# Last expert of a mixture-of-experts block: all weight blocks over three token tiles, then all over two

## What is computed

```python
capacity = max(1, int(CF * N / E))                       # 640
disp = jnp.zeros((E, capacity + 1, D)).at[se, pos].set(xf[st])[:, :capacity]
g = jnp.einsum('ecd,edf->ecf', disp, wg)                 # D = 256, F = 1024
u = jnp.einsum('ecd,edf->ecf', disp, wu)
eo = jnp.einsum('ecf,efd->ecd', jax.nn.silu(g) * u, wd)
contrib = gathered * (sw * keep)[:, None]
out = jnp.zeros_like(xf).at[st].add(contrib)             # x = x + gate * out
```

## Time and profile before

| | us |
|---|---|
| median of 3 runs | 678.95 (678.22 to 679.12) |
| the profiled execution's own time | 678.13 |
| its span, first to last instruction | 676.04 |
| TensorE busy | 568.7 (84%) |
| VectorE busy | 456.5 (68%) |
| ScalarE busy | 320.0 (47%) |
| GpSimd busy | 269.0 (40%) |

### The profile page before, as it was taken

The page is one execution under the profiler, slowest core; times in us unless marked ns, Lnnn a source line. Parts: engine busy times, 40 slices in busy tenths (PEclk is TensorE's granted clock), DMA queues, the critical chain, the costliest instruction groups (busy, mean ns, idle before and its releaser), DMA issues.

```text
span 676.0 us, 13788 instructions
## 1 busy us (share of the span) xinstructions
PE 568.7 (84%) x4041; PEld 529.4 (78%) x4041; DVE 456.5 (68%) x1304; ACT 320.0 (47%) x717; POOL 269.0 (40%) x427
## 2 busy tenths in 40 slices
PE   4999889998997101279999999999999999999990
PEld 3577668887776000169999999999999999999990
DVE  3577889897677877867756766567667666666431
ACT  3688778886444500034534534445345444454330
POOL 5688757776678000302007025043070160442304
PEclk9999999999999555569989999999999999999996
DMA  5322268545554900144408317344174073340203
GB/s 164 94 64 78 71 194 264 189 145 162 157 190 153 264 0 0 40 133 133 133 1 213 94 44 170 95 141 102 61 198 106 18 194 95 110 102 9 32 1 39
DMA packets 91911, 75.24 MB, mean 111 GB/s; under 512 B 12108, under 2 KB 88278, under 8 KB 91864
## 3 DMA queue, kind: packets, MB, share of 16 engines
q1 hardware_dynamic: 82872, 58.77, 28.6%
q0 software_dynamic: 8992, 15.90, 11.2%
HBM read 52.48 MB, written 22.16 MB: 110 GB/s over the span
## 4 chain that ended last, share of the span: by engine, by line
PE 59%; DVE 13%; issue 7%; POOL 3%; ACT 2%; DMA 2%; DVEq 1%; SPq 0%; ACTq 0%; POOLq 0%
PE bank L1329 33%; PE bank L1341 15%; PE bank L1247 3%; PE bank L1292 2%; DVE hit L880 2%; PE bank L1150 2%; PE bank L1306 1%; DMA mod_all<-mod_store 1%; DVE x L847 1%; DVE st L849 1%; POOL out L506 1%; PE bank L1227 1%; PE bank L1236 1%; DMA xg<-h_rows,g_idx 1%; PE bank L1202 0%
## 5 line engine op out<-in xcount | busy, mean ns | idle before, releaser
L1329 PE MATMUL bank<-xT_h,w_h 128*128 128x320 f32 x512 | 160.2, 313 | 2.3 <-DVE xT_l L1027 1.7
L1329 PE MATMUL bank<-xT_l,w_h 128*128 128x320 f32 x512 | 159.2, 311 | 0.4 <-issue 0.4
L1329 PE MATMUL bank<-xT_h,w_l 128*128 128x320 f32 x512 | 159.0, 311 | 0.0
L496 POOL DMA_INDIRECT xg<-h_rows,g_idx x40 | 43.8, 1095 | 274.5 <-DVE g_idx L999 264.7
L1055 DVE TENSOR_TENSOR hid<-act_g,bank 128x320 f32<-128x320 f32 x128 | 62.0, 484 | 74.1 <-ACT act_g L648 59.6
L652 ACT CAST hid_h<-hid 128x320 fp32r<-128x320 f32 x128 | 58.9, 460 | 97.5 <-DVE hid L1055 92.8
L648 ACT ACTIVATE act_g<-bank 128x320 f32<-128x320 f32 x128 | 55.8, 436 | 103.3 <-PE bank L1329 96.2
L1329 PEld LDWEIGHTS bank<-xT_h,w_h 128*128 128x128 f32 x512 | 97.6, 191 | 3.0 <-DVE w_l L1013 2.1
L1329 PEld LDWEIGHTS bank<-xT_h,w_l 128*128 128x128 f32 x512 | 97.5, 190 | 0.5 <-issue 0.5
L1329 PEld LDWEIGHTS bank<-xT_l,w_h 128*128 128x128 f32 x512 | 97.5, 190 | 0.5 <-issue 0.5
L1341 PE MATMUL bank<-w_h,hid_h 128*128 128x256 f32 x320 | 91.4, 286 | 0.4 <-DVE hid_l L1060 0.4
(11 more groups left out here) (180 smaller groups left out, 1118.2 us busy)
## 6 DMA issues: line engine op xcount, KB each, us to landing
w_raw<-wg SPq DMA_DIRECT2D x32, 256.0 KB, 3.3
w_raw<-wu SPq DMA_DIRECT2D x32, 256.0 KB, 4.4
w_raw<-wd SPq DMA_DIRECT2D x16, 512.0 KB, 6.1
x_in<-x SPq DMA_DIRECT2D x32, 128.0 KB, 2.1
q_store<-qT SPq DMA_DIRECT2D x32, 128.0 KB, 1.9
q_in<-q_store SPq DMA_DIRECT2D x32, 128.0 KB, 2.2
x_re<-x SPq DMA_DIRECT2D x32, 128.0 KB, 2.2
out<-x SPq DMA_DIRECT2D x32, 128.0 KB, 1.9
```

The lines of the kernel that those rows point to most:

```text
L496: nc.gpsimd.indirect_dma_start(out=xg[par][:, a, :], out_offset=None, in_=h2_rows, in_offset=bass.IndirectOffsetOnAxis(ap=g_idx[par][:, a: ...
L1329: last = MM(bank[2 * h + m][:, 0:HCAP], W[i][:, f, at:at + P], XT[j][:, k, cols], start=n == 0, stop=n == 3 * KC - 1)
```

## The change

Only the last expert changes. Its token tiles are taken in two parts, tiles 0 to 2 and tiles 3 and 4 (`PARTS`), and each part goes through all eight weight blocks. A step `j` from 0 to 15 is one block of one part: steps 0 to 7 are part 0, with gate/up matmuls of 384 columns and a down product of three tiles, steps 8 to 15 are part 1, with 256 columns and two tiles. There are no halves any more; the two sets of banks and buffers alternate by step.

On TensorE, gate/up of step `j` is followed by down of step `j - 1` up to step 8; gate/up 9 comes alone, and from step 10 on down of step `j - 2` follows. The last three down products (13, 14, 15) stand at the end; so the program has three down products of two tiles behind its last gate/up group. Tiles 3 and 4 have a bank each, 6 and 7, and a semaphore of their own, `y_last`, which goes up after each of the two tiles.

On VectorE all five tiles of expert 6 are weighed ahead of the first `hid_l`. Tiles 0 to 2 of expert 7 are weighed behind `hid_l` of step 9, tiles 3 and 4 at the end. GpSimd and SP have the same instructions as before. `act_g` and `hid` become 384 columns wide.

```diff
 HCAP = CAP // 2
+PARTS = ((0, 3), (3, CT))
+WIDE = 3 * P
...
-        act_g = [sb(f"act_g{i}", [P, HCAP]) for i in range(2)]
-        hid = [sb(f"hid{i}", [P, HCAP]) for i in range(2)]
+        act_g = [sb(f"act_g{i}", [P, WIDE]) for i in range(2)]
+        hid = [sb(f"hid{i}", [P, WIDE]) for i in range(2)]
...
+        def last_y(a):
+
+            return (bank[4][:, 0:D], bank[4][:, D:2 * D], bank[5][:, 0:D], bank[6][:, 0:D], bank[7][:, 0:D])[a]
...
+            def last_expert(e):
+
+                for j in range(2 * FC):
+                    lo, hi = PARTS[j // FC]
+                    n, i, h = (hi - lo) * P, e * 2 * FC + j, j % 2
+                    act.wait_ge(gu_d, i + 1)
+                    act.wait_ge(hid_d, i - 1)
+                    nc.scalar.activation(act_g[h][:, 0:n], bank[2 * h][:, 0:n], ACT.Silu).then_inc(silu_d, 1)
+                    act.wait_ge(hid_d, i + 1)
+                    act.wait_ge(dn_d, e * FC + j - 1)
+                    nc.scalar.copy(hid_h[h][:, 0:n], hid[h][:, 0:n]).then_inc(hh_d, 1)
+                    if j < 2:
+                        split_high(e, FC - 2 + j, e * FC + FC - 2 + j, implied=True)
+
+            last_expert(E - 1)
...
+            def weigh_last(e, par, a):
+
+                V.scalar_tensor_tensor(yo[:, a, :], last_y(a), w_slot[par][:, a:a + 1], xg[par][:, a, D:2 * D],
+                                       ALU.mult, ALU.mult).then_inc(ym_d, 1)
+
+            def last_expert(e, par):
+
+                for j in range(2 * FC):
+                    lo, hi = PARTS[j // FC]
+                    n, i, h = (hi - lo) * P, e * 2 * FC + j, j % 2
+                    dve.wait_ge(silu_d, i + 1)
+                    dve.wait_ge(hh_d, i - 1)
+                    V.tensor_tensor(hid[h][:, 0:n], act_g[h][:, 0:n], bank[2 * h + 1][:, 0:n], ALU.mult).then_inc(hid_d, 1)
+                    if j == 0:
+                        weigh(e - 1, 1 - par)
+                    if j == 3:
+                        find_targets(e, par)
+                    if j == 4:
+                        find_weights(e, par)
+                        dve.wait_ge(ws_d, e + 1)
+                    dve.wait_ge(hh_d, i + 1)
+                    V.tensor_tensor(hid_l[h][:, 0:n], hid[h][:, 0:n], hid_h[h][:, 0:n].bitcast(F32), ALU.subtract)\
+                        .then_inc(hl_d, 1)
+                    if j < 2:
+                        split_low(e, FC - 2 + j, e * FC + FC - 2 + j)
+                    if j == FC + 1:
+                        dve.wait_ge(sc_d, e * CT * 16 + 16)
+                        dve.wait_ge(dn_d, e * FC + FC)
+                        for a in range(*PARTS[0]):
+                            weigh_last(e, par, a)
+                for a in range(*PARTS[1]):
+                    dve.wait_ge(y_last, a - PARTS[1][0] + 1)
+                    weigh_last(e, par, a)
+
+            last_expert(E - 1, (E - 1) % 2)
...
+            def last_gate_up(e, par, j):
+
+                W, XT = (w_h, w_l), (xT_h[par], xT_l[par])
+                (lo, hi), f, h = PARTS[j // FC], j % FC, j % 2
+                pe.wait_ge(sp_l, e * FC + f + 1)
+                if j == 0:
+                    pe.wait_ge(xl_d, e * XG + XG)
+                pe.wait_ge(hid_d, e * 2 * FC + j - 1)
+                for m in range(2):
+                    n = 0
+                    for k in range(KC):
+                        for i, x in PASSES:
+                            at = (2 * m + k) * P
+                            last = MM(bank[2 * h + m][:, 0:(hi - lo) * P], W[i][:, f, at:at + P],
+                                      XT[x][:, k, lo * P:hi * P], start=n == 0, stop=n == 3 * KC - 1)
+                            n += 1
+                last.then_inc(gu_d, 1)
+
+            def last_down(e, j):
+
+                (lo, hi), f, h = PARTS[j // FC], j % FC, j % 2
+                pe.wait_ge(hh_d, e * 2 * FC + j + 1)
+                pe.wait_ge(hl_d, e * 2 * FC + j + 1)
+                if j == 0:
+                    pe.wait_ge(ym_d, e * CT)
+                for a in range(lo, hi):
+                    for n, (i, x) in enumerate(PASSES):
+                        last = MM(last_y(a), (hid_h, hid_l)[x][h][:, (a - lo) * P:(a - lo + 1) * P],
+                                  (w_h, w_l)[i][:, f, 4 * P:], start=f == 0 and n == 0 and a != 1,
+                                  stop=f == FC - 1 and n == 2, skip_group_check=True)
+                    if j == 2 * FC - 1:
+                        last.then_inc(y_last, 1)
+                if j < 2 * FC - 1:
+                    last.then_inc(dn_d, 1)
...
+                if then_last:
+                    last_gate_up(e + 1, 1 - par, 0)
+                    down(e, FC - 1)
+                    return
+                gate_up(e + 1, 1 - par, 0)
                 down(e, FC - 1)
-                if not last:
-                    gate_up(e + 1, 1 - par, 1)
-                    down(e + 1, 0)
...
+            def last_expert(e, par):
+
+                for j in range(1, FC + 1):
+                    last_gate_up(e, par, j)
+                    last_down(e, j - 1)
+                last_gate_up(e, par, FC + 1)
+                for j in range(FC + 2, 2 * FC):
+                    last_gate_up(e, par, j)
+                    last_down(e, j - 2)
+                last_down(e, 2 * FC - 2)
+                last_down(e, 2 * FC - 1)
```

More of the change, by code:

```diff
@@ L638, in _, with expert @@
                 x_high(0, 0, g, bk=g)
-            def expert(e, par, first=False, last=False):
+            def expert(e, par, first=False):
                 xf = FC - XG if first else XF
@@ L651, in expert @@
                             wait(act, dn_d, e * FC + f - 1)
-                        nc.scalar.copy(hid_h[f % 2][:, h * HCAP:(h + 1) * HCAP], hid[h][:, :]).then_inc(hh_d, 1)
-                    if not last and xf <= f < xf + XG:
+                        nc.scalar.copy(hid_h[f % 2][:, h * HCAP:(h + 1) * HCAP], hid[h][:, 0:HCAP]).then_inc(hh_d, 1)
+                    if xf <= f < xf + XG:
                         x_high(e + 1, 1 - par, f - xf)
@@ L657, in expert @@
                         split_high(e, FC - 2 + f, e * FC + FC - 2 + f, implied=True)
-                    elif not last:
+                    else:
                         split_high(e + 1, f - 2, e * FC + FC + f - 2)
@@ L664, in _ @@
                 expert(k * 2 + 2, 0)
-            expert(E - 1, 1, last=True)
+            def last_expert(e):
[11 more added lines that the diff above has]
+            last_expert(E - 1)
         @block.vector
@@ L1046, in weigh, with expert @@
                                            w_slot[par][:, a:a + 1], xg[par][:, a, D:2 * D], ALU.mult, ALU.mult).then_inc(ym_d, 1)
-            def expert(e, par, first=False, last=False, ahead=True):
+            def expert(e, par, first=False, ahead=True):
                 def hidden(f, h):
@@ L1082, in expert @@
                         weigh(e - 1, 1 - par, 0, 2)
-                    if f == (3 if first else 1) and not last:
+                    if f == (3 if first else 1):
                         find_tokens(e + 1, 1 - par)
@@ L1119, in _ @@
                 expert(k * 2 + 2, 0)
-            for e in range(E - 3, E):
-                expert(e, e % 2, last=e == E - 1, ahead=e + 2 < E)
-            for a in range(CT):
-                weigh(E - 1, (E - 1) % 2, a, a + 1)
+            for e in range(E - 3, E - 1):
+                expert(e, e % 2, ahead=e + 2 < E)
+            def weigh_last(e, par, a):
[29 more added lines that the diff above has]
+            last_expert(E - 1, (E - 1) % 2)
         @block.tensor
@@ L1347, in down, with expert @@
                 last.then_inc(dn_d, 1)
-            def expert(e, par, first=False, last=False, ahead=True):
+            def last_gate_up(e, par, j):
[29 more added lines that the diff above has]
+                    last.then_inc(dn_d, 1)
+            def expert(e, par, first=False, ahead=True, then_last=False):
                 xf = FC - XG if first else XF
@@ L1361, in expert @@
                         look(e + 2)
-                if not last:
-                    gate_up(e + 1, 1 - par, 0)
+                if then_last:
[3 more added lines that the diff above has]
+                gate_up(e + 1, 1 - par, 0)
                 down(e, FC - 1)
-                if not last:
-                    gate_up(e + 1, 1 - par, 1)
-                    down(e + 1, 0)
+                gate_up(e + 1, 1 - par, 1)
+                down(e + 1, 0)
             gate_up(0, 0, 0, first=True)
@@ L1375, in _ @@
                 expert(k * 2 + 2, 0)
-            for e in range(E - 3, E):
-                expert(e, e % 2, last=e == E - 1, ahead=e + 2 < E)
+            for e in range(E - 3, E - 1):
+                expert(e, e % 2, ahead=e + 2 < E, then_last=e == E - 2)
+            def last_expert(e, par):
[8 more added lines that the diff above has]
+                last_down(e, 2 * FC - 1)
+            last_expert(E - 1, (E - 1) % 2)
```

8 lines of the change are left out of this document (4 added, 4 removed).

## The result

The changed kernel takes 674.84 us as the median of 7 runs (673.59 to 677.16), the kernel before 679.12 (678.22 to 681.04, 7 runs beside them). The ratio is 0.994 with a 95% interval of 0.9924 to 0.9956, so it is faster by 3 to 5 us, and 674.1 had been forecast. The profiled execution took 675.54 with a span of 673.6; that of before 678.13 with 676.04.

What follows compares the result with a forecast made beforehand. The last expert runs at TensorE's pace, then a tail waits for GpSimd's five scatters. -5.60 + 0.78 = -4.82 us gave 673.3, and 674.1 with the 0.8 between median and profiled run; range 672.9 to 676.0.

Steps and rivals of the forecast that it cites:

- Scatters, -5.60: GpSimd's tail: two scatters follow the last down product in place of five, 3 x 1.865 = -5.60 us.
- TensorE's stream, -0.22: Last expert's gate/up matmuls at 384 and 256 columns take 27.87 us in place of 28.09 at 320, -0.22.
- Behind the last group: After the last gate/up group, 18 down matmuls (2.08 us) replace 30 (3.46); its last matmul issues 1.17 later.
- The chain, 1.91 at 256 columns: ScalarE and VectorE path from gate/up group's end to down product: 1.91 us; TensorE idles about 0.7 before the last down.
- New waits: New TensorE stalls inside the last expert: 0.15 between the parts and 0.05 at its start, otherwise none.
- The seam: Between the two parts, a 256-column group covers 2.24 us of a 2.39 chain: one stall of 0.15.
- The front: Start of the last expert: down 0 may start at 621.33, TensorE arrives at 621.31; 0.05 taken, bounds 0 and 0.5.
- First `yo` of the tail, +0.78: Tile 3's `yo` starts at 659.76 against 658.98 for the tail's first `yo` before, +0.78 us.
- GpSimd then needs the same 0.8: From the tail's first `yo` to its scatter's issue GpSimd takes 0.8 us, as before; tile 4's scatter follows 1.865 later.
- (a): Rival: weight loads hold narrow matmuls, 256-column pitch 0.187 in place of 0.115, +6.9 us or 681.0; 3%.
- (b): Rival: TensorE waits in every step of part 0 because the 384-column chain is longer, +2.1 or 676.2; 6%.
- (c): Rival: tail not shortened as said; time behind last issue differs or the pair's first scatter starts late, up to 3.5; 3%.

Runs made afterwards that it cites:

- the two-and-three split: Changed kernel with two tiles in the first part and three in the second; 57.9 us from the last expert's first gate/up matmul to the end.
- a lag of one: Changed kernel with part 1's down product one step behind its gate/up, not two; 57.9 us from the last expert's first gate/up matmul to the end.
- the second profile: The changed kernel once more, unchanged; medians 672.08 against 675.92 us for the kernel before, ratio 0.9929.
- the swap: Tile 4 ahead of tile 3 on all engines, on the kernel with three down products between last gate/up group and down 15; ratio 0.9921 to the kernel before.
- the gather: One more tile gather before expert 7's scatters, on the kernel with three down products between last gate/up group and down 15; ratio 0.9926 to the kernel before.

## Why the prediction was right, point by point

1. *Scatters, -5.60.* Shown. Putting them back costs all of the gain, at the pitch of 1.865. Three scatters ran from 650.03 to 655.3, covered by part 1.
2. *TensorE's stream, -0.22.* The pitches were right: 2.09 us for 12 matmuls of 384 columns, 1.36 to 1.41 for 256. A whole step of part 0 came to 3.14 (624.21 to 627.35) as reckoned, and one of part 1 to 2.09 on the mean (649.14 to 657.50 are four) in place of 2.07. About 0.1 of the 0.22 was kept, which is too little to tell anything by.
3. *Behind the last group.* Three down products of two tiles stand there, and the group ended its issue 41.70 us after the last expert's first matmul (TensorE's next down product starts at 658.75, less 617.05), against 41.36 + 0.20 of the prediction, so 0.14 late.
4. *The chain, 1.91 at 256 columns.* 660.83 - 658.93 = 1.90. The idle 0.7 us was there; the run with three down products ahead of down 15 shows that it was real time on the path, and `yo` 3 comes 0.5 to 0.6 earlier there (0.8 in the two later profiles of that order).
5. *New waits.* The seam: 1.21 in place of 1.06, so 0.15, as written. No stall in the other steps. The front, which I called a tie:

```profile
622.81 0.34 PE L1417 MATMUL bank<-xT_h,w_l 128*128 128x384 f32 x1
622.99 0.31 PE L1431 MATMUL bank<-w_h,hid_h 128*128 128x256 f32 x1
```

   0.18 from start to start where the pitch is 0.174: the tie is one, and the two-and-three split shows what lies behind it. The three `yo` of part 0 held up nothing; with a lag of one they cost 0.3.
6. *First `yo` of the tail, +0.78.* It is 661.46 - 617.05 = 44.41 against 658.98 - 615.38 = 43.60, so +0.81. That this is so close is in part luck, since two misses cancel in it: the last group was 0.14 late (part 3), and from down 15 to `yo` it took 661.46 - 660.83 = 0.63, not the 0.73 that came of taking three matmuls off the 1.08.
7. *"GpSimd then needs the same 0.8."* This is the step that failed. From the end of `yo` 3 to its scatter it took 1.58, not 0.8, which costs 0.79 us and recurs in all profiles in which this scatter finds GpSimd free. I took the price from first scatters of a group, and this is a fourth. Without it the change would have brought 4.9 us to the end, where I had forecast 4.8.

Together: -5.60 + 0.81 + 0.79 - 0.13 (6.63 in place of 6.76 behind the last issue, 673.6 - 666.97) = -4.1, which is what the two spans give.

The size was therefore missed by 0.7 us and stayed in the range. The absolute number owes something to luck too: beside the runs of the second profile the kernel before took 675.92 and the changed one 672.08, which is below the range although the gain is of the same size. It is the difference that was forecast, not the level.

Of the rivals, (a) didn't come: 256 columns ran at 0.115. But it is nearer than I gave it room for: the floor of matmuls with an f32 weight load each lies at 0.1075, and the rows of 8 columns in the trace before could have told so. (b) didn't come. (c) was right in one half that I had put at 3%: the first of the pair starts late, though not because of idling, and at 0.8 us, not 3.5.

What stays open is why the fourth scatter of the last group is 0.8 us slower to leave. It is in GpSimd's own sequencer, between two increments that elsewhere are 0.55 us apart. In the profile of before the same pair has 1.35 us between its increments (661.16 and 662.51), and the time was hidden since GpSimd was busy with scatter 0 and 1 then; with all five `yo` in the tail it is the same (657.82 and 659.17). Four instructions more, a DMA more ahead or behind, a gather more and another tile in its place changed nothing, and the fourth scatter of expert 6 has 0.56. Not tried: a shift by a known number of instructions as long as a scatter's or longer, the last group in a loop, or another expert's group behind it.

The best version of this study is the one with three down products between the last gate/up group and the last down, 56.0 to 56.1 us to the end in three profiles (two of them with the swap or the gather) against 56.55 to 56.8 for the change as it was made and with small additions.

## What to carry to other kernels

Where the end of a kernel is a row of equal jobs on a slow engine that had idled before, it pays to let part of its input finish early, even if the faster engine then works through the same loop twice: all of the gain here is the three scatters that no longer stand in the tail. Work out before it what the narrower pieces cost (a matmul with an f32 weight load of its own has a floor of about 0.11 us here) and what stands behind the last long group, for there a chain of 1.9 us is only as cheap as what covers it. And compare two profiles from the last point at which they are still the same: the whole spans gave 2.4 us here, the stretch behind that point 4.1, in line with the medians.

## What was not expected of the hardware

- Matmuls of 128 columns with an f32 weight load each run at 0.1075 us, and of 8 columns at 0.118, though at 256 to 512 columns the pitch is 0.45 ns a column (0.115 at 256, 0.174 at 384, 0.229 at 512). With bf16 operands and 10 columns it is 0.063.
- The fourth scatter of the last group leaves GpSimd 0.8 us later than the first scatters of groups do, in all ten profiles in which it opens the tail. Why is open.
- Behind the last scatter's issue lie 6.63 us in the changed kernel and 6.76 before; with one scatter in the tail it is 6.75, with three 6.75 and with five 6.85. So the first half of rival (c) is answered: this stretch doesn't depend on how many stand there. 4.11 us of it are GpSimd's DRAIN behind the program's last wait (669.25 to 673.36 in the changed kernel, 671.70 to 675.81 before), and it is 4.11 to 4.20 in every profile.
